# Attention outputs turned by VectorE's block transposes, and layer statistics of two batches from one instruction, in a fused attention block

## What is computed

```python
x_norm = modulate(_ln(x), shift_a, scale_a)
q, k, v = split(x_norm @ W_qkv + b_qkv)            # 16 heads of 8
attn_out = softmax(q @ k.T * scale) @ v            # per batch and head
x = x + gate_a * (attn_out @ W_proj + b_proj)
q_c = _ln(x) @ W_qc + b_qc
k_c, v_c = split(_ln(context) @ W_kvc + b_kvc)
x = x + softmax(q_c @ k_c.T * scale) @ v_c @ W_cproj + b_cproj
h = gelu(modulate(_ln(x), shift_m, scale_m) @ W_mlp1 + b_mlp1) @ W_mlp2 + b_mlp2
x = x + gate_m * h
```

## Time and profile before

| what | value |
|---|---|
| three runs | 406.55, 407.51 and 403.11 us, median 406.55 us |
| profiled execution, first to last instruction (span) | 401.9 us |
| its own device time | not given with the profile; the runs lie 1.2 to 5.6 us above its span |
| PE busy | 336.8 us, 84% |
| ACT, DVE, POOL busy | 268.8, 257.0, 216.6 us |
| steady slots (some 16.4 us each) | from about 119 to 260 us of the span |
| MLP alone | from about 340 us on |

### The profile page before, as it was taken

The page is one execution under the profiler, slowest core; times in us unless marked ns, Lnnn a source line. Parts: engine busy times, 40 slices in busy tenths (PEclk is TensorE's granted clock), DMA queues, the critical chain, the costliest instruction groups (busy, mean ns, idle before and its releaser), DMA issues.

```text
span 401.9 us, 16368 instructions
## 1 busy us (share of the span) xinstructions
PE 336.8 (84%) x6072; PEld 227.1 (56%) x6072; DVE 257.0 (64%) x650; ACT 268.8 (67%) x523; POOL 216.6 (54%) x494
## 2 busy tenths in 40 slices
PE   3474875989889999999999899988678778999994
PEld 3342553666666767667677677766545434454442
DVE  5754665768779788788887888868625441424401
ACT  1244563868778888887888878877573465677672
POOL 7824475867676686777777777756344210211200
PEclk9997799999999999999999999999997599999998
DMA  5244467253343543435425343353130300001101
GB/s 154 52 105 108 125 151 166 55 136 85 85 97 82 119 106 81 102 85 126 99 68 123 81 116 94 81 123 78 36 82 4 81 2 2 26 26 41 39 26 52
DMA packets 65549, 33.15 MB, mean 82 GB/s; under 512 B 8359, under 2 KB 65255, under 8 KB 65511
## 3 DMA queue, kind: packets, MB, share of 16 engines
q1 hardware_dynamic: 61983, 31.77, 32.7%
q10 hardware_dynamic: 3528, 0.86, 1.1%
HBM read 4.83 MB, written 2.10 MB: 17 GB/s over the span
## 4 chain that ended last, share of the span: by engine, by line
PE 41%; DVE 16%; issue 16%; SPq 9%; DMA 8%; ACT 4%; POOL 2%; ACTq 1%; DVEq 1%; POOLq 0%
PE ps_o L1180 7%; DMA qkc_st<-qkcp 7%; SPq L372 7%; PE ps_o L1133 6%; PE wide L1172 6%; PE wide L1111 5%; DVE x_n L714 3%; PE wide L1122 3%; DVE mxc L736 3%; DVE mx L736 2%; SPq L412 2%; DVE x_stats L698 2%; PE ps_misc L1200 2%; PE ps_misc L1208 2%; PE ps_misc L1221 2%
## 5 line engine op out<-in xcount | busy, mean ns | idle before, releaser
L895 ACT ACTIVATE p_c<-wide 128x1024 f32<-128x1024 f32 x64 | 65.6, 1026 | 36.5 <-PE wide L1122 36.1
L736 DVE TENSOR_REDUCE mx<-wide 128x8 f32<-128x1024 f32 x64 | 78.0, 1218 | 18.4 <-PE wide L1111 18.2
L895 ACT ACTIVATE p_s<-wide 128x1024 f32<-128x1024 f32 x64 | 65.7, 1026 | 11.8 <-PE wide L1122 11.0
L736 DVE TENSOR_REDUCE mxc<-wide 128x8 f32<-128x616 f32 x64 | 51.0, 797 | 27.5 <-PE wide L1111 26.4
L1133 PE MATMUL ps_o<-p_c,vc_m 128*32 128x128 f32 x1024 | 43.0, 287 | 0.8 <-ACT p_c L895 0.6
L1133 PE MATMUL ps_o<-p_s,v_m 128*32 128x128 f32 x1024 | 42.5, 285 | 0.6
L1111 PE MATMUL wide<-qk_st 62*128 62x128 bf16 x512 | 26.5, 225 | 11.6 <-DVE mx L736 9.7
L1111 PE MATMUL wide<-qkc_st 62*128 62x77 bf16 x512 | 20.8, 204 | 14.2 <-DMA qkc_st<-qkcp 13.4
L1111 PEld LDWEIGHTS wide<-qk_st 62*128 62x128 bf16 x512 | 15.1, 97 | 29.3 <-DVE mx L736 23.7
L1133 PEld LDWEIGHTS ps_o<-p_s,v_m 128*32 128x32 f32 x1024 | 25.1, 111 | 8.4 <-issue 3.1
L1172 PE MATMUL wide<-m_nT,w_sb 128*128 128x512 f32 x64 | 29.6, 597 | 0.2 <-DVE mxc L736 0.2
(11 more groups left out here) (152 smaller groups left out, 815.5 us busy)
## 6 DMA issues: line engine op xcount, KB each, us to landing
qkc_st<-qkcp SPq DMA_DIRECT2D x96, 128.0 KB, 2.6
qk_st<-qkp SPq DMA_DIRECT2D x94, 128.0 KB, 2.5
out<-m_out SPq DMA_DIRECT2D x8, 256.0 KB, 2.3
xs<-x SPq DMA_DIRECT2D x3, 512.0 KB, 4.9
qk_st<-nmT SPq DMA_DIRECT2D x64, 4.0 KB
qkc_st<-nmcT SPq DMA_DIRECT2D x64, 4.0 KB
ctx_sb<-ctx SPq DMA_DIRECT2D x3, 308.0 KB
w_sb<-L_xcond_W_mlp ACTq DMA_DIRECT2D x2, 256.0 KB, 3.1
```

The source lines that it names most:

```text
L736: nc.vector.reduce_max(mxt[:, b].rearrange("q (x r) -> q r x", r=2)[:, r], src, AX.X, negate=True).then_inc(sems[done], 1)
L895: nc.scalar.activation(dst[u % 2][:].rearrange("k x q -> k (x q)"), ps_st[:].rearrange("k s x -> k (s x)"), ACT.Exp, scale=SCALE).then_inc ...
```

## The change

- The self and cross outputs no longer pass through ACT and PE. `turn_sums` on DVE transposes the 32 x 32 blocks of `ps_o` straight from PSUM to SBUF (128 x 512 elements; beat 1 or 5, behind the maxima of the beat, ahead of the statistics of x1). `divide` takes the reciprocal and multiplies, now from SBUF to SBUF (beat 2 or 6, behind the maxima and ahead of the normalisation of x1). `turn_back` transposes the blocks of the result (128 x 256, SBUF to SBUF) into oT or ocT (top of beat 3 or 7, before the maxima).
- ACT's `sums` and the two copies of oT and ocT go; PE's `flip_sums` and `flip_out` go with their four places in MISC.
- `values` puts its units at other columns of `ps_o`, and `w_proj`, `w_cproj` and the value biases are loaded in their plain order, in one DMA each.
- `stats` makes one `bn_stats` over the two batches with their elements interleaved (the inner step between elements is a whole batch, 128 floats); the engine's separate statistics of even and odd elements are then those of the two batches. `aggregate` goes; POOL turns the sum of squares into the variance and adds epsilon in one `tensor_scalar`. In the MLP two such instructions take the place of four `bn_stats` and four `bn_aggr`.

```diff
 MISC = [("max_c1", "back3", 0), ("proj_c", "back4", 1),
         ("qk", "ahead", 0),
-        ("max_s0", "here", 2), ("o_t", "back1", 1),
-        ("ob_t", "back1", 2), ("ctx_t", "back1", 0), ("v", "ahead", 1),
+        ("max_s0", "here", 2),
+        ("ctx_t", "back1", 0), ("v", "ahead", 1),
...
@@ SP, loads
-            for r in range(2):
-                sp.dma_start(wcproj_sb[r * C // 2:(r + 1) * C // 2], o_rows(w_cproj)[r]).then_inc(sems["w_in"], 16)
+            sp.dma_start(wcproj_sb[:], w_cproj).then_inc(sems["w_in"], 16)
@@ POOL, rstd
-                w(pool, f"{kind}_mv_set", p.n + 1)
-                nc.gpsimd.tensor_tensor(L["ve"][:], L["mv"][:, :, 1], eps_sb[0:L["rows"], 0:G],
+                hold(pool, f"{kind}_stats_set", p.n + 1)
+                nc.gpsimd.tensor_scalar(L["ve"][:], L["stats"][:, :, 2], 1.0 / C, EPS, ALU.mult,
                                         ALU.add).then_inc(sems[f"{kind}_ve_set"], 1)
@@ DVE
             def stats(kind, p, src):
-                L = ln[kind]
-                for b in range(G):
-                    last = nc.vector.bn_stats(L["stats"][:, b], src(b))
-                last.then_inc(sems[f"{kind}_stats_set"], 1)
-
-            def aggregate(kind, p):
-...
+                if not p.first():
+                    hold(dve, f"{kind}_n_set", p.n)
+                nc.vector.bn_stats(ln[kind]["stats"][:].rearrange("t b k -> t (b k)"),
+                                   interleaved(src[:, batches(p)])).then_inc(sems[f"{kind}_stats_set"], 1)
...
-            def attention_out(p, kind, job, ready, rden_name, name, taken):
-...
+            def turn_sums(p, kind, ready, name):
+
+                w(dve, ready, NU * p.n + NU)
+                nc.vector.transpose(att[kind]["sum"][:].rearrange("t (a r s) x -> t a r (s x)", r=2, s=2),
+                                    ps_o[:].rearrange("c (r a q) -> c a r q", r=2, q=32)).then_inc(sems[name], 1)
+
+            def divide(p, kind, ready, rden_name, name):
+
                 w(dve, ready, p.n + 1)
+                nc.vector.reciprocal(att[kind]["rden"][:], att[kind]["sum"][:, :, D]).then_inc(sems[rden_name], 1)
+                w(dve, rden_name, p.n + 1)
+                nc.vector.tensor_tensor(att[kind]["o"][:], att[kind]["sum"][:, :, 0:D],
+                                        att[kind]["rden"][:].unsqueeze(2).to_broadcast([128, 2 * G * T // 16, D]),
+                                        ALU.mult).then_inc(sems[name], 1)
+
+            def turn_back(p, kind, dst, ready, name, taken):
+
+                w(dve, ready, p.n + 1)
                 if not p.first():
                     w(dve, taken, p.n)
-...
+                nc.vector.transpose(dst[:], att[kind]["o"][:].rearrange("t m d -> t (m d)")).then_inc(sems[name], 1)
@@ DVE, slot
                     if t == 3 and d:
-                        attention_out(d, "s", "o_t", "ot_ps", "rden_set", "o_set", "obt_ps")
+                        turn_back(d, "s", oT, "o_set", "oT_set", "proj_ps")
                     if t == 7 and e:
-                        attention_out(e, "c", "oc_t", "oct_ps", "rdenc_set", "oc_set", "obct_ps")
+                        turn_back(e, "c", ocT, "oc_set", "ocT_set", "projc_ps")
...
+                    if t == 1 and d:
+                        turn_sums(d, "s", "pv_ps", "sum_set")
+                    if t == 2 and d:
+                        divide(d, "s", "sum_set", "rden_set", "o_set")
+                    if t == 5 and e:
+                        turn_sums(e, "c", "pvc_ps", "sumc_set")
+                    if t == 6 and e:
+                        divide(e, "c", "sumc_set", "rdenc_set", "oc_set")
@@ ACT, slot
-                    if t == 0 and z:
-                        copy(ocT[:], ps_misc[BANK["obc_t"]][:, 0:GT], "obct_ps", z, "ocT_set", "projc_ps")
...
-                    if t == 1 and d:
-                        sums(d, "s", ps_o, "pv_ps", "sum_set", "ot_ps")
...
-                    if t == 5 and e:
-                        sums(e, "c", ps_o, "pvc_ps", "sumc_set", "oct_ps")
@@ PE
                 b, r = divmod(u, 2)
-                at = u * T
+                at = (G * r + b) * T
...
-                    if t == 2 and d:
-                        flip_sums("o_t", "s", d, "sum_set", "ot_ps")
...
-                        flip_out("ob_t", "s", d, "o_set", "obt_ps")
...
-                    if t == 6 and e:
-                        flip_sums("oc_t", "c", e, "sumc_set", "oct_ps")
...
-                    if t == 7 and e:
-                        flip_out("obc_t", "c", e, "oc_set", "obct_ps")
```

More of the change, by code:

```diff
@@ L325, in block_kernel @@
         for kind in ln:
-            for what in ("stats", "mv", "ve", "rstd", "n"):
+            for what in ("stats", "ve", "rstd", "n"):
                 sem(f"{kind}_{what}_set")
@@ L565, in m_rstd_step @@
             def m_rstd_step(g):
-                w(pool, "m_mv_set", g + 1)
-                nc.gpsimd.tensor_tensor(m_ve[:], m_mv[:, :, 1], eps_sb[:, 0:MG], ALU.add).then_inc(sems["m_ve_set"], 1)
+                hold(pool, "m_stats_set", g + 1)
+                nc.gpsimd.tensor_scalar(m_ve[:], m_stats[:, :, 2], 1.0 / C, EPS, ALU.mult,
+                                        ALU.add).then_inc(sems["m_ve_set"], 1)
                 w(pool, "m_ve_set", g + 1)
@@ L693, in gate_rows, with interleaved @@
                 nc.vector.tensor_copy(g_rows[0:3, 2], rows[0:3, 3 * C:4 * C]).then_inc(sems["g_set"], 1)
+            def interleaved(pair):
+                return pair.rearrange("t b c -> t c b")
             def stats(kind, p, src):
-                L = ln[kind]
-                for b in range(G):
-                    last = nc.vector.bn_stats(L["stats"][:, b], src(b))
-                last.then_inc(sems[f"{kind}_stats_set"], 1)
-            def aggregate(kind, p):
-                L = ln[kind]
-                hold(dve, f"{kind}_stats_set", p.n + 1)
-                for b in range(G):
-                    last = nc.vector.bn_aggr(L["mv"][:, b], L["stats"][:, b])
-                last.then_inc(sems[f"{kind}_mv_set"], 1)
+                if not p.first():
+                    hold(dve, f"{kind}_n_set", p.n)
+                nc.vector.bn_stats(ln[kind]["stats"][:].rearrange("t b k -> t (b k)"),
+                                   interleaved(src[:, batches(p)])).then_inc(sems[f"{kind}_stats_set"], 1)
             def normalise(kind, p, src, taken):
@@ L766, in m_norm @@
                     hold(dve, "m_n_set", g)
-                for b in range(MG):
-                    last = nc.vector.bn_stats(m_stats[:, b], one(g, b))
+                for b in range(0, MG, 2):
+                    at = bass.ds(MG * g + b, 2) if not isinstance(g, int) else slice(MG * g + b, MG * g + b + 2)
+                    last = nc.vector.bn_stats(m_stats[:, b:b + 2].rearrange("t b k -> t (b k)"), interleaved(xs[:, at]))
                 last.then_inc(sems["m_stats_set"], 1)
-                hold(dve, "m_stats_set", g + 1)
-                for b in range(MG):
-                    last = nc.vector.bn_aggr(m_mv[:, b], m_stats[:, b])
-                last.then_inc(sems["m_mv_set"], 1)
                 if not first and not (isinstance(g, int) and g < 2):
@@ L777, in m_norm @@
                 for b in range(MG):
-                    last = nc.vector.tensor_scalar(m_n[par][:, b], one(g, b), m_mv[:, b, 0:1], m_rstd[:, b:b + 1],
+                    last = nc.vector.tensor_scalar(m_n[par][:, b], one(g, b), m_stats[:, b, 1:2], m_rstd[:, b:b + 1],
                                                    ALU.subtract, ALU.mult)
@@ L908, in empty_max @@
                 nc.scalar.activation(dst[:, b], ps_misc[BANK[job]][:].bitcast(bf16)[0:2 * H, 0:T],
-                                     ACT.Copy).then_inc(sems[name], 1)
-            def sums(p, kind, src, ready, name, taken):
-                w(act, ready, NU * p.n + NU)
-                if not p.first():
-                    w(act, taken, p.n)
-                nc.scalar.activation(att[kind]["sum"][:].rearrange("c b r q -> c (b r q)"), src[:, :],
                                      ACT.Copy).then_inc(sems[name], 1)
@@ L995, in slot @@
                     if t == 4 and d:
-                        copy(oT[:], ps_misc[BANK["ob_t"]][:, 0:GT], "obt_ps", d, "oT_set", "proj_ps")
-                    if t == 4 and d:
                         copy(cT[:], ps_misc[BANK["ctx_t"]][:, 0:GS], "ctxt_ps", d, "cT_set", "kvc_ps")
```

79 lines of the change are left out of this document (25 added, 54 removed).

## The result

The changed kernel takes 418.49 us, median of four runs (417.30 to 420.07); the kernel before 404.83 us (402.14 to 407.51), median of four runs too. The ratio is 1.0336, 95% interval 1.0277 to 1.0396: the change makes the kernel 13.6 us slower. (Some executions of a kernel come out over 1.5% above its fastest one: ratios and intervals leave these out, medians do not.) The profiled execution took 420.07 us with a span of 418.3, so 1.8 us lie around the span.

The account below looks back on a forecast made before the run. The prediction took a loop through all engines, closed by the DMA, to bound the kernel. 14 slots x 0.76 = +10.6, less 2.0 where slots end, gave +8.6 on the 406.55 median: 415.0 us, range 397 to 426.

Parts of the forecast that it names:

- The loop through x1, SP and the DMA: Steady slots: a loop through all engines, closed by the DMA, sets the 16.4 us slot; delaying x1 on DVE moves the rest.
- PE's relief: Rival, beats 1 to 3 and 6: less work on PE decides, 14 x -0.7 - 2 = -12, 395 us; chance 0.2.
- Durations on DVE: Prices on DVE: turn 0.61 us, turn_back 0.34, divide 0.81, each statistics step 0.46 less.
- the collisions that I kept for the range: DVE's divide multiply, two SBUF inputs, against POOL: 0 in the sum, 0.3 us a slot kept for the range.
- +0.96 on x1's way: DVE, maxima of beat 5 to x1: cross turn +0.61, statistics -0.46, cross divide +0.81 us a slot.
- -0.2 at SP, so +0.76 a slot: Between q_c and SP's stack DMAs: earlier nmcT wins at most 0.2 us, leaving +0.76 a slot, +10.6 over 14.
- The other half of the slot has 0.3 us of cover: Beat 0's to beat 4's scores: about 8.1 us, under the 8.4 of nmcT, SP and DMA.
- -2.0 where the slots end: Where slots end: DVE's three steps replace waits and transposes, saving 0.60 + 0.58 + 0.31 + 0.56 = 2.0 us.
- That PE's clock falls with its lower load I leave out: PE's clock: no fall priced, as the granted clock was 1.00 in the slot read.
- Cancelling: Rival: turns and divide at lower ends, more won at SP; 14 x 0.2 - 2 = +1, 407 us; chance 0.17.
- Slow 32-bit transposes: Rival: slow transposes on DVE, or POOL's port holding the divide; 2.2 us a slot, +29, 435 us; chance 0.13.

Follow-up runs that it names:

- The delay runs: Kernel before plus one DVE transpose of unread elements ahead of x1's normalisation: 352 elements 1.0082, 409.22 us; 768 elements 1.0384, 419.39 us.
- the self turn alone: Kernel before with the new statistics and only the self output turned on DVE: 0.9997, 404.2 us with more rounds.
- the statistics alone: Kernel before with only the new statistics, outputs turned by PE as before: 0.9874, 400.47 us; with more rounds 0.9924, 402.6 us.
- x1 first: Changed kernel with x1's statistics ahead of the cross turn and x1's normalisation ahead of the cross divide: 1.0000, 407.23 us.
- cross alone: Kernel before with the new statistics and only the cross output turned on DVE, its divide behind x1's normalisation: 1.0004.
- the turns alone: Changed kernel with the old statistics put back, so only the outputs are changed: 1.0893, 439.7 us.
- the filled kernels: Unread matmuls added ahead of PE's transposes: changed kernel 1.0359, 418.78 us; the same with x1's steps ahead of cross turn and divide 1.0102, 408.16 us.
- the smaller delay: Kernel before plus one DVE transpose of 352 unread elements ahead of x1's normalisation: 1.0082, 409.22 us.

## Why the prediction was right, and where a step was off

The forecast was 415.0 us, slower with a chance of 0.59, from 397 to 426. It came out slower, at 418.5. As a difference the forecast was +8.6 us, and +13.6 was measured. Point by point:

- *The loop through x1, SP and the DMA bounds the kernel, and PE's relief is worth nothing there.* Right in the undisturbed slots. PE lost 1.4 us of work a slot and its idle time ahead of x_n grew by about as much. The delay runs show the mechanism without the change.
- *Durations on DVE.* The groups of the kernel after (busy us, mean ns, idle before), which answer to the earlier trace rows:

```profile
L732 DVE STREAM_TRANSPOSE c_sum<-ps_o 128x512 f32<-128x512 f32 x16 | 11.4, 710 | 8.5 <-PE ps_o L1113 8.5
...
L740 DVE TENSOR_TENSOR s_o<-s_sum,s_rden 128x256 f32<-128x256 f32 x16 | 9.8, 611 | 0.5
...
L749 DVE STREAM_TRANSPOSE ocT<-c_o 128x256 f32<-128x256 f32 x16 | 7.0, 438 | 0.1
L740 DVE TENSOR_TENSOR c_o<-c_sum,c_rden 128x256 f32<-128x256 f32 x16 | 6.8, 427 | 0.5
...
L695 DVE BATCH_NORM_STATS2 x_stats<-xs 128x6 f32<-128x256 f32 x12 | 4.9, 412 | 0.1
```

  The turn was put at 0.61 occupied and measured 0.63; turning back was put at 0.34 and takes 0.44 from start to end; one bn_stats was put at 0.41 and took 0.412. The divide was put at 0.81 and takes 0.72. Of the penalty in the Trainium skill, Advanced Engine Details and Errata, "SBUF Cachelines", these rows show nothing: 256 elements read at a stride of 512 bytes cost 0.13 us more than the 128 contiguous ones of the earlier trace rows, which is the rate of any 128 more elements. The mean of s_o went from 425 to 611 ns with both inputs in SBUF, its longest to 1291; the rule of the Trainium skill, SBUF — State Buffer, "Who interferes with whom", agrees with that. c_o, at the critical place, stayed at 427; there it was POOL's ctx_rstd, started 0.03 us behind it, that took 0.96 us (0.70 before). POOL still stood idle for 0.54 us ahead of its cast of q_c, so the collisions that I kept for the range did not fall on the loop.
- *+0.96 on x1's way.* Measured +0.88 to x1's normalisation and +0.87 to PE's transpose of it.
- *-0.2 at SP, so +0.76 a slot.* This term was mis-sized: the slot grew by 0.45. The reason given for the 0.2 (SP must first issue the single stack DMA) was right in order, and up to the last issue 0.11 was won. But the landing, which the forecast left as it was, is 0.28 shorter (2.39 instead of 2.67 us), so the stretch from q_c's start to the landing is 0.39 shorter (8.72 against 9.11). 0.88 - 0.39 is the slot's difference to a few hundredths.
- *The other half of the slot has 0.3 us of cover.* No run shows it late in an undisturbed slot; the self turn alone leaves the slot at 15.92. So it does not enter.
- *-2.0 where the slots end.* Wrong in sign. From the last cross scores to the end it takes 85.6 us, 84.3 before. The three steps on DVE did come sooner, but PE was then in the middle of MLP work. DVE's and PE's timelines, kernel after:

```profile
352.90 0.45 DVE L749 STREAM_TRANSPOSE ocT<-c_o 128x256 f32<-128x256 f32 x1
```

```profile
355.79 0.29 PE L1268 MATMUL ps_misc<-g_rows,ones 128*32 128x256 bf16 x4
```

  The output lay ready at 353.35 and PE came for it 2.4 us later. From the last values to this projection it is 4.6 us, 5.7 before; the stretch from the last cross scores to the last values is 2.3 us longer, with the clock at 0.84 from 340 to 350 us, where before it was 1.00 in the like stretch (325 to 335).
- *"That PE's clock falls with its lower load I leave out."* This is the weakest step, though not for the reason that it names. One steady slot at 1.00 was read, and the rest of the run was taken to be like it, late landings and stretches at half speed at nothing. Three dips in the slots before 200 us, at some 1.5 us each, are the part of it that a row prices; whether the lower load brings them is not shown, since the statistics alone have one as well. The slots were priced 4.3 us too high (0.31 x 14), and all that lies outside them, put at -2.0, came to 13.6 - 6.3 = +7.3. So 415.0 came near 418.5 partly by luck, through two errors of opposite sign.

The rivals: relief of PE does not decide in any kernel here. Cancelling is what x1 first does, not the change. Slow 32-bit transposes are ruled out by their durations.

What stays open: what makes the turned kernels 3.5 to 8 us slower than their undisturbed slots. The profile after shows both late landings in the hardware loop's first turn and stretches of PE at half speed, of which one begins behind a late landing and two behind the wait for x1. The mean clock over all executions is 0.954 with the statistics alone and 0.958 and 0.963 with the delays, near the 0.955 to 0.959 of the kernel before, and lower with every turned kernel: 0.947 self alone, 0.938 cross alone, 0.931 x1 first, 0.930 after, 0.897 the turns alone. That goes with their excess but does not prove the clock its cause: the filled kernels have 1.00 in the middle and are no faster in the median. Nor is it known why a landing is late in the loop's first turn. In the filled kernel it took 2.39 us there, and that slot was 17.55 us long all the same, with one of SP's issues at 1.47 instead of 0.62 us. A kernel with PE's load lowered and nothing added to DVE was not tried.

## What to carry to other kernels

Before moving work from the busiest engine to another, follow the chain that ended last and ask what is queued on the receiving engine behind the new instructions: here the order of DVE's list alone, the cross divide and the turn ahead of x1's own instructions or behind them, was worth some 10 us in the slots and 13 in all. When an edit has two parts, time each alone; here one of them (statistics of two batches in one instruction) was worth 0.8% and the other hid it. One quiet slot tells what the loop costs, but before the forecast is multiplied out, look at the slots that are longer than the rest, at the landing that each waits for and at the granted clock in them.

## What the runs showed of the hardware that I had not expected

- DVE's 32-bit block transposes take about 1 ns for each further element of a row: 128 x 256, 352 and 768 elements from SBUF took 0.44, 0.53 and 0.96 us, and 128 x 512 from PSUM took 0.71.
- x1's normalisation (two instructions of 128 x 128, one SBUF input each) took 0.57 to 0.70 us as a pair in its usual place, 0.89 in the kernel with the 768-element delay and 0.97 in the turns alone. It is the same work, moved by some tenths against POOL's; what it collides with was not tried.
- The DMA of the stacked queries and keys landed after 2.4 to 2.7 us in steady slots and after 3.4 to 4.1 us in the first slot of the hardware loop, in kernels without filler. In the kernels with turned outputs without filler the second slot had it as well, 3.5 to 3.9 us, where before, the statistics alone and both delays had 2.4 to 2.6. Late landings came again in the slots behind the loop's end, in some executions and not in others: 4.29 us with x1 first, 3.91 with the smaller delay, 2.6 before.
